# The second piece of the first weights, issued by ScalarE instead of SyncE

## What is computed

```python
xn = layernorm(x)
g  = sigmoid(xn @ gate_w.T + gate_b); u_g = xn * g
y  = c * G * cumsum(b * u_g / G) + (d + low_rank(mean(u_g))) * u_g   # G = cumprod(tanh(a))
h  = silu(xn @ w1.T); h = silu(h @ w3.T); h = h @ w2.T
out[indices_k] += gates_k * h        # indices are expert numbers 0..7, top 2 of 8
return x + y * silu(out)
```

## Time and profile before

| | us |
|---|---|
| median of 3 runs | 730.83 (730.68 to 730.86) |
| the profiled execution, whole | 730.16 |
| its span, first to last instruction | 728.3 |
| TensorE busy | 723.7 (99%) |
| VectorE busy | 517.9 (71%) |
| ScalarE busy | 357.7 (49%) |
| DMA: bytes moved | 126.81 MB, mean 174 GB/s |

### The profile page before, as it was taken

How to read it: one execution, slowest core, us unless ns; L and a number is a source line. 1 busy time by engine, 2 the same in 40 slices (tenths; PEclk the granted TensorE clock), 3 DMA queues, 4 the chain that set the end, 5 groups by cost and what they waited for, 6 DMA issues and landing times.

```text
span 728.3 us, 10078 instructions
## 1 busy us (share of the span) xinstructions
PE 723.7 (99%) x4194; PEld 601.8 (83%) x4194; DVE 517.9 (71%) x508; ACT 357.7 (49%) x447; POOL 21.3 (3%) x34
## 2 busy tenths in 40 slices
PE   9999999999999999999999999999999999999998
PEld 8888888888888888888888888888888888888887
DVE  5988467758675786699989987357588756885522
ACT  6648849255755675354924553324244441463221
POOL 0000000002010010000000000000000000000000
PEclk9999999999999999999999999999999999999999
DMA  8616835678365847869676803341138103300140
GB/s 336 252 58 230 296 154 197 243 265 289 116 234 168 295 142 265 289 217 332 218 274 230 317 3 144 129 161 51 39 125 307 58 1 145 144 2 1 55 181 4
DMA packets 31118, 126.81 MB, mean 174 GB/s; under 512 B 4760, under 2 KB 4952, under 8 KB 23904
## 3 DMA queue, kind: packets, MB, share of 16 engines
q1 hardware_dynamic: 21824, 109.37, 42.2%
q10 hardware_dynamic: 9248, 16.80, 6.3%
HBM read 105.08 MB, written 37.78 MB: 196 GB/s over the span
## 4 chain that ended last, share of the span: by engine, by line
PE 99%; DVE 0%; ACT 0%; issue 0%
PE main L949 31%; PE main L950 31%; PE main L951 31%; PE lgp L1028 2%; PE lgp L1041 1%; PE spare L1041 1%; PE spare L956 1%; PE main L978 0%; PE main L981 0%; PE main L984 0%; PE lgp L1055 0%; PE main L1055 0%; DVE tail L1102 0%; ACT u L939 0%; DVE lg L1437 0%
## 5 line engine op out<-in xcount | busy, mean ns | idle before, releaser
L1102 DVE TENSOR_TENSOR s<-s,main 128x512 f32<-128x512 f32 x72 | 48.6, 682 | 63.2 <-PE main L951 63.2
L1102 DVE TENSOR_TENSOR u<-u,main 128x512 f32<-128x512 f32 x36 | 24.3, 683 | 35.2 <-PE main L951 35.2
L805 ACT ACTIVATE s<-main 128x512 f32<-128x512 f32 x36 | 20.9, 593 | 44.4 <-PE main L951 21.9
L830 ACT ACTIVATE rows<-rows 128x512 f32<-128x512 f32 x16 | 10.0, 632 | 65.4 <-DVE rows L1102 65.4
L1102 DVE TENSOR_TENSOR u<-s,main 128x512 f32<-128x512 f32 x32 | 21.6, 684 | 24.8 <-PE main L951 24.8
L751 ACT ACTIVATE rows<-rows,nm 128x1024 f32<-128x1024 f32 x32 | 36.9, 1153 | 1.0
L749 ACT ACTIVATE rows<-rows 128x1024 f32<-128x1024 f32 x32 | 33.6, 1049 | 5.4 <-DMA rows<-x 4.3
L830 ACT ACTIVATE s<-s 128x512 f32<-128x512 f32 x24 | 15.0, 630 | 42.3 <-DVE s L1102 42.3
L830 ACT ACTIVATE u<-u 128x512 f32<-128x512 f32 x24 | 15.1, 628 | 29.3 <-DVE u L1102 29.3
L1102 DVE TENSOR_TENSOR rows<-s,main 128x512 f32<-128x512 f32 x16 | 10.8, 685 | 21.8 <-PE main L951 21.8
L950 PE MATMUL main<-x7r,wh2r 128*128 128x512 f32 x48 | 18.7, 389 | 0.0
(11 more groups left out here) (656 smaller groups left out, 2374.3 us busy)
## 6 DMA issues: line engine op xcount, KB each, us to landing
rows<-x SPq DMA_DIRECT2D x32, 512.0 KB, 4.7
out<-x SPq DMA_DIRECT2D x31, 512.0 KB, 10.2
H_d<-u ACTq DMA_DIRECT2D x32, 256.0 KB, 4.6
H_d<-s ACTq DMA_DIRECT2D x16, 256.0 KB, 5.0
bc<-mv_d SPq DMA_DIRECT2D x8, 512.0 KB, 4.3
rows<-w SPq DMA_DIRECT2D x8, 512.0 KB, 5.2
rows<-xh_d SPq DMA_DIRECT2D x16, 256.0 KB, 5.3
w2f<-w2T SPq DMA_DIRECT2D x2, 2048.0 KB, 10.0
```

The source lines that it names most:

```text
L805: eng.activation(s1[:, j, :], bk, ACT.Copy).then_inc(s_pa, 1)
L830: eng.activation(c, c, ACT.Silu).then_inc(s_sl, 1)
L1102: return eng.tensor_tensor(o, a, b, op)
```

## The change

SyncE's loop leaves out weight piece 1 of block `a`. ScalarE issues it: after its first tiny activation it waits for the landing of input piece 0, issues the same transfer to the same tile with the same semaphore, and goes on as before.

```diff
@@ SyncE, first loop
             for b in "ac":
                 for k in range(PIECES[b]):
                     first_block(b, k)
-                    first_weights(b, k)
+                    if (b, k) != ("a", 1):
+                        first_weights(b, k)
@@ ScalarE, start
             on.wait_ge(s_po, 1)
             eng.activation(nm[:, :], mhalf[:, 0:1], ACT.Silu)
+            on.wait_ge(s_x0["a"][0], 16)
+            eng.dma_start(part(w_from(0, 0), "a", 1), w11[1]).then_inc(s_w0["a"][1], 16)
```

## The result

The changed kernel takes 733.49 us (median of 7 runs, 732.30 to 734.61) against 730.80 for the kernel before (7 runs, 730.42 to 731.03). The ratio is 1.0038, 95% interval 1.0028 to 1.0047: slower by 2.7 us, clear of noise. I had forecast 730.9 us and a range up to 731.8. The profiled execution took 733.52 us, its span is 731.7.

What follows compares the result with a forecast made beforehand. TensorE, busy 723.7 of 728.3 us, was taken as the bound, with only its first microseconds movable. Issue costs and savings counted 0, the later landing +0.1: median 730.83 + 0.1 = 730.9 us, range 730.3 to 731.8.

Steps and rivals of the forecast that it cites:

- The reading of the bound: At TensorE's start of k=1 (7.53 us), a later start reaches the end one for one; weight piece 1 has 0.05 us spare.
- The issue on ScalarE: ScalarE's new wait and issue at about 3.46 us, hidden by the wait for weight piece 0: cost 0.
- SyncE's issue saved: On SyncE, all later issues start 0.47 us earlier, worth nothing because those transfers wait for the DMA engines.
- the landing of the moved transfer: Weight piece 1 from ScalarE's queue lands at 6.91 us against 6.74; ScalarE starts it +0.17 later, taken as +0.1.
- The thin stretch of the engines: DMA engines busy for only 0.57 at 3.5 to 3.75 us, a reason to expect a landing near the lower end.
- D: Rival: the piece queues behind everything SyncE issued by 3.46, landing 8.26 to 8.86; +1.5 to 2.1 us, chance 0.05.
- B: Rival: input piece 1 lands early without competition and TensorE's 0.23 us pause before k=1 vanishes; 730.6 us, chance 0.15.
- The cover at k=2 and at block `c`: On TensorE, no second pause: k=2's difference done at 9.44, needed at 10.18; `c` blocks land where they did.

Runs made afterwards that it cites:

- second profile: The changed kernel run and profiled again with no edit: 732.75 us, ratio 1.0034 to the kernel before.
- e2: Changed kernel, but SyncE too waits for input piece 0 before issuing input piece 2: 731.50 us, ratio 1.0020.
- e8: Kernel before, but ScalarE issues weight piece 0 as its very first instruction and SyncE the rest: 730.61 us, ratio 1.0000.
- e3: Kernel before, but SyncE issues weight piece 1 itself, eighth, behind weight piece 3, with no ScalarE issue or new wait: 733.39 us, ratio 1.0040.
- e7: Changed kernel with eight more warming products on TensorE between the first and second piece: 732.54 us, ratio 1.0029.
- e4: Changed kernel with ScalarE's wait moved to the landing of input piece 1: 738.49 us, ratio 1.0105.
- e5: Kernel before, all issued by SyncE in the old order, but SyncE waits for input piece 0 before issuing weight piece 1: 731.63 us, ratio 1.0013.
- e9: Changed kernel, but SyncE waits for weight piece 0 before issuing input piece 2: 731.90 us, ratio 1.0024.
- e1: Changed kernel without the new wait ahead of ScalarE's issue of weight piece 1: 731.68 us, ratio 1.0017.

## Why the prediction was wrong

**The reading of the bound was right.** Weight piece 1 had 0.05 us to spare ahead of 7.53, and a delay there reaches the end one for one: 3.50 us at k=1 and 3.4 in the span in the first profile, 2.67 and 2.6 in the second.

**The issue on ScalarE costs nothing: right.** 0.39 us, from 3.67 to 4.06, and weight piece 0 was rounded at 4.30, when it had landed (3.1 us after its issue at 1.23). That this is 0.23 later than before comes from the landings, since input piece 0 was late by the same amount in that execution; it was covered.

**SyncE's issue saved: right, worth nothing.** Input piece 2 is issued 0.47 us earlier and piece 1's rounding does not move.

**The step that failed is the landing of the moved transfer.** I took 2.8 + 0.65 us from the first transfers on idle engines plus one turn of sharing, landing at 6.91; it took 5.9 and 6.6 us, landing at 9.43 and 10.26. I gave two reasons for standing near the lower end, and both were bad. The thin stretch of the engines at 3.5 to 3.75 us (0.57 busy) I read as room for a newcomer; but when ScalarE issued in the changed kernel, seven transfers had been issued and 1.58 - 1.07 = 0.51 MB moved, two pieces (1.58 MB is what SyncE's queue had moved by 7.10). So work was waiting, and the thin stretch was no room for a newcomer: in the first profile the same quarter of a microsecond read 0.80 and the next 0.94, and not one packet of ScalarE's was among them. And I took the sharing between queues, which does take place (e2, e8, from 7.10 us on in the changed kernel), for a right to be let in at once. It begins only with the second queue's first packet.

The Trainium skill ("DMA: Bandwidth & Descriptors", section "Queues, rings and completion order") has each DMA engine take turns between queues with work. The first profile agrees from the first packet on, with 213 and 137 packets of the two queues in 2 us, and shows 0 packets of the second queue in the 3.43 us before it. The sentence of the Trainium skill (the same page, section "Issuing engines are not separate DMA queues") that another issuing engine saves only issue time was the better guide: e3 measures the same loss with no second engine at all.

**The rivals.** D was the right mechanism in the main, with a chance of 0.05, and its price was too small: I bounded the landing by 5.4 us, the wait of a SyncE piece issued at 4.04, while in the changed kernel the piece issued at 3.57 took 5.9 and ScalarE's 6.6. The rows for D were in the prediction (4.8 and 5.4 us for pieces issued around that time); with them the likeliest landing was 8.3 to 8.9 us, not 6.9. D's 1.5 to 2.1 us became 3.5 (6.79 to 10.29, first profile) and 2.7 (6.79 to 9.45, second profile) at the rounding of the piece, and 2.7 and 2.2 by the two medians. B, an earlier input piece 1, did not come in these two profiles: rounded at 6.22 and 6.42 against 6.12. But in e7, with the same transfers, it was rounded at 5.05:

```profile
5.05 0.63 ACT L758 ACTIVATE x2r<-x0f 128x512 fp32r<-128x512 f32 x1 [0.20 <-DMA x0f<-xa]
```

So B's first half can happen, by its own mechanism or by chance, and wins nothing while weight piece 1 lands at 8.25. The further cost that D named, a clock that falls with the pause, was seen in the profiles of e3 and e4, in neither of the changed kernel's.

**The cover at k=2 and at block `c` held**: no second pause in the changed kernel. It was wrong to think it ample, as e5 shows, where the `c` loads were issued 1.0 to 1.5 us later, the second input piece of `c` landed 2.3 us later (15.7 against 13.4), and TensorE paused for 1.9 us. In e9, with issues as late, that piece landed at 14.7 and the pause was 0.2.

## What to carry to other kernels

In this kernel a transfer moved to an idle engine's queue got ahead of little that the busy one had already issued. Count the transfers issued before it and not yet landed, and price it like the next one on the busy queue (here 5.4 us from the rows, against 4.8 to 6.6 measured), with a range of a microsecond on each side. Moving a transfer to a later moment cost the places it lost, and not only the issue times between. Where two transfers were both needed early, one queue in the order of need landed the first one sooner than two queues together (e8, one profile). And read a single profile of such a start with care: three executions that issue the same transfers landed this piece at 8.25, 9.43 and 10.26.

## What was not expected of the hardware

- A DMA issue written behind an activation on ScalarE went out at 0.87 us, during the table load (0.74 to 2.02) and before that activation (2.03), when no semaphore stood between them (e1).
- Two 256 KB loads issued together on two queues landed after 3.7 and 3.9 us, against 2.7 and 2.8 when issued 0.49 us apart on one (e8).
- The first four matmuls of k=0 took 2.04 us in the changed kernel and 1.25 before, although the granted-clock column reads 1.00: the warming matmuls' end and the start of k=0 lay 0.29 us apart there. The pause covered it. Why full speed came later I leave open, since in e2 and e7 it also came late (1.35 us for the four loads, as there) with no such gap. In e1, after a gap of 0.95 us, the next four loads were slow too (1.61), with the column still at 1.00 up to 9 us, and nothing covered it; from 10 us on the column read 0.95 there, and four matmuls took 1.07 to 1.09 us, no longer than at 1.00.
